# Cross attention: the next half's exponentials ahead of rounding on ScalarE, its normalisation ahead of splitting on VectorE

## What is computed

```python
q_r = einsum('bshq,hqr->bhsr', rope((layernorm(x) @ Wq.T) @ w_kc_q), W_qr)
k_r = einsum('bld,hdr->bhlr', kv_r, W_kr)          # kv_r: the rotated context
attn = softmax(einsum('bhsr,bhlr->bhsl', q_r, k_r), axis=-1)
ctx_c = einsum('bhsl,bld->bhsd', attn, kv_r)
x = x + (einsum('bhsd,hkd->bhsk', ctx_c, w_kc_kv) -> heads side by side) @ Wo.T
```

## Time and profile before

| | us |
|---|---|
| median of 3 runs | 1657.17 |
| lowest, highest | 1654.75, 1658.53 |
| the profiled execution's own time | 1657.46 |
| its span | 1655.7 |
| TensorE busy in the span | 1485.7 (90%) |
| VectorE, ScalarE, GpSimd busy | 1126.5, 810.0, 541.2 |

### The profile page before, as it was taken

The page is one execution under the profiler, slowest core; times in us unless marked ns, Lnnn a source line. Parts: engine busy times, 40 slices in busy tenths (PEclk is TensorE's granted clock), DMA queues, the critical chain, the costliest instruction groups (busy, mean ns, idle before and its releaser), DMA issues. The chain is left out here.

```text
span 1655.7 us, 26391 instructions
## 1 busy us (share of the span) xinstructions
PE 1485.7 (90%) x8136; PEld 1127.4 (68%) x8136; DVE 1126.5 (68%) x1814; ACT 810.0 (49%) x1723; POOL 541.2 (33%) x594
## 2 busy tenths in 40 slices
PE   5799999999946999999999978999899499999996
PEld 3577777777634777777777767887444277777775
DVE  6788878787435878788787854777558436474646
ACT  4556665666423555555555534555210355545453
POOL 4235424341024454545545413220131402221202
PEclk9899999999968999999999998999899699999998
DMA  4132433423267353445444404000444000000000
GB/s 156 59 104 82 126 103 106 125 76 111 78 170 247 106 127 103 120 109 120 112 117 111 129 20 166 0 0 1 154 176 153 0 1 1 26 1 25 1 26 26
DMA packets 140459, 143.78 MB, mean 87 GB/s; under 512 B 83441, under 2 KB 103025, under 8 KB 138737
## 3 DMA queue, kind: packets, MB, share of 16 engines
q1 hardware_dynamic: 138672, 133.87, 27.6%
q10 hardware_dynamic: 1728, 9.20, 1.7%
HBM read 113.54 MB, written 29.49 MB: 86 GB/s over the span
## 5 line engine op out<-in xcount | busy, mean ns | idle before, releaser
L942 ACT ACTIVATE c_e_t_high<-c_et_ps 128x512 fp32r<-128x512 f32 x128 | 76.7, 599 | 227.2 <-PE c_et_ps L1011 227.2
L820 POOL TENSOR_TENSOR c_mixed_low<-c_whole,c_mixed_high 128x512 fp32r<-128x512 f32 x64 | 95.6, 1494 | 178.6 <-ACT c_mixed_high L954 178.6
L77 DVE TENSOR_TENSOR b_rot_parts_low<-b_rot,b_rot_parts_high 128x1536 fp32r<-128x1536 f32 x64 | 135.8, 2122 | 21.8 <-ACT b_rot_parts_high L526 21.8
L1003 PE MATMUL c_sc_ps<-c_kv_t,c_q 128*128 128x257 f32 x512 | 137.1, 392 | 15.1 <-DMA c_q<-carried_queries 15.1
L843 DVE TENSOR_REDUCE c_peak<-c_sc_ps 128x2 f32<-128x514 f32 x128 | 88.5, 691 | 55.7 <-PE c_sc_ps L1003 55.0
L264 POOL TENSOR_TENSOR b_turned_raw<-b_turn_part 128x384 f32<-128x384 f32 x32 | 70.1, 2189 | 166.1 <-DVE b_key_parts_low L77 164.8
L1003 PEld LDWEIGHTS c_sc_ps<-c_kv_t,c_q 128*128 128x128 f32 x512 | 100.1, 197 | 34.5 <-DMA c_q<-carried_queries 15.9
L70 PE MATMUL e_mm_ps<-folded_high,e_h_t_high 128*128 128x512 f32 x256 | 108.8, 425 | 15.8 <-DVE e_h_t_low L77 15.6
L309 DVE TENSOR_TENSOR b_rot<-b_w_qr,b_angle 128x1536 f32<-128x1536 f32 x64 | 119.2, 1863 | 0.2
L1515 PE MATMUL f_ps<-f_right,f_left 128*128 128x512 f32 x256 | 112.6, 602 | 7.3 <-POOL spare L1487 5.0
L934 ACT ACTIVATE c_e<-c_sc_ps,c_peak 128x257 f32<-128x257 f32 x256 | 118.8, 475 | 0.0
(11 more groups left out here) (210 smaller groups left out, 3953.3 us busy)
## 6 DMA issues: line engine op xcount, KB each, us to landing
c_q<-carried_queries SPq DMA_DIRECT2D x64, 256.0 KB, 3.7
c_ends_spread<-end_weights SPq DMA_DIRECT2D x64, 256.0 KB, 4.4
carried_queries<-x SPq DMA_DIRECT2D x7, 2048.0 KB, 11.2
b_early<-early SPq DMA_DIRECT2D x15, 640.0 KB, 4.0
c_raw<-cache_t SPq DMA_DIRECT2D x64, 128.5 KB, 3.9
c_swapped<-cache_t SPq DMA_DIRECT2D x128, 64.2 KB, 3.9
f_left<-ent_in SPq DMA_DIRECT2D x16, 512.0 KB, 5.5
f_right<-ent_out SPq DMA_DIRECT2D x16, 512.0 KB, 6.8
```

Source lines behind the costliest of these rows:

```text
L77: return nc.vector.tensor_tensor(low, value, high.bitcast(F32), ALU.subtract)
L820: nc.gpsimd.tensor_tensor(mixed[1][:, w, :, u], whole[:, u % 2].rearrange("p (h s) -> p h s", h=H), mixed[0][:, w, :, u].bitcast(F32), ALU ...
L1003: last = nc.tensor.matmul(sc_ps[:, 2 * half + c, 0:L], q[:, u, at], kv_t[:, u], start=True, stop=True)
```

## The change

Two calls are moved, each within its engine's step. No instruction, wait or buffer is added or removed. On VectorE `normalise(n + 1)` goes from behind `split_turned(n)`, `split_kv` and `add_out` to ahead of them. On ScalarE `exponential(n + 1)` goes ahead of `round_turned(n)`.

```diff
--- before.py
+++ after.py
@@ -891,13 +891,13 @@
                         find_peak(n + 1, 1 - half)
                     if half == 1 and (u or known(i, 1)):
                         add_end(i - (u == 0), (u - 1) % BT)
+                    if more:
+                        normalise(n + 1, 1 - half)
                     split_turned(n, u, half)
                     if half == 0:
                         split_kv(b, u)
                     if j == 2 and known(i, 2):
                         add_out(i - 2)
-                    if more:
-                        normalise(n + 1, 1 - half)
                     if j == 4 and known(i, 2):
                         keep_moments(i - 2)
 
@@ -967,9 +967,9 @@
                 for j in range(STEPS):
                     n, u, half = STEPS * i + j, j // 2, j % 2
                     b = BT * i + u
-                    round_turned(n, b, u, half)
                     if not (isinstance(n, int) and n == PAIRS - 1):
                         exponential(n + 1, 1 - half)
+                    round_turned(n, b, u, half)
                     if half == 0:
                         round_kv(b, u)
                     if half == 1 and (u or known(i, 1)):
```

## The result

The changed kernel takes **1653.36 us** (median of 20 runs, 1650.56 to 1655.69) against 1657.39 before (median of 20 runs beside it): a ratio of 0.9976, interval 0.9969 to 0.9983, so 4.0 us faster, between 2.8 and 5.1. Forecast were 1651 us and 6.6 us. The profiled execution took 1651.63 us, its span is 1649.8. Two of the 20 executions of before took 2194 and 2195 us and one of even_only's 2807; such slow executions are in the medians and in no ratio.

A forecast was written before the change was run, and what follows sets the result against it. TensorE was taken to set the pace, losing 1.69 us per tile waiting ahead of odd steps' transposes. A gain of 0.47 x 14 = 6.6 us from 1657.46 gave 1651 us, range 1645 to 1661 (8 in 10).

The forecast's parts named there:

- the stall of j = 3: Wait ahead of j = 3's transposes, 0.99 us before; forecast to move to j = 4 as 0.76.
- the walk: Step-by-step clocking of the engines from a step's scores; gave 1.34 us lost per tile before, 1.06 after.
- first case: Stall moves from j = 3 to j = 4, small waits change sides: gain 4.5 to 10.1 us, chance 0.67.
- a new wait of 0.10: Ahead of even steps' transposes, which odd steps' VectorE chain makes 0.10 us late.
- the base of 28.12: Length in us of a tile's four even and four odd steps undisturbed, against 29.81 measured.
- the middle between 0.32 and 0.63: Gain per tile, 0.47 us: 0.32 if lengthened products stay as costly, 0.63 if no longer in the way.
- the 0.31: Loss per tile in us beyond the 1.38 accounted for, put down to lengthened products of line 850.
- the third rival: Even steps' product hits GpSimd's line 803 soon after it begins: slower, deciding from overlap 0.36; chance 0.11.
- The spare of 0.06: VectorE's margin in us in even steps: free that much before the next peaks are wanted.
- The second: Rival: 0.10 more lateness in each of four odd steps leaves 1 us gain, 1656; chance 0.15.
- The fourth: Rival: walk too strict for add_out, TensorE's gaps close: 24 us gain, 1633; chance 0.07.

The follow-up runs named there:

- even_only: Changed kernel with the new order in even steps alone, odd steps in the old order on VectorE and ScalarE: 1649.74 us, ratio 0.9958 to the kernel before.
- act_only: Kernel before with ScalarE's move alone, exponential ahead of round_turned: 1735.34 us, ratio 1.0464.
- dve_only: Changed kernel with ScalarE's two calls as before, so VectorE's move alone: 1687.36 us, ratio 1.0178 to the kernel before.
- wait_swap: Changed kernel with TensorE's two waits ahead of the transposes swapped, low part first: 1652.20 us, ratio 0.9971 to the kernel before.
- wait_first: Changed kernel with those two TensorE waits swapped and an always-met wait for the pair's scores ahead: 1652.85 us, ratio 0.9975 to the kernel before.
- gap_after: Changed kernel with add_out right behind find_peak at j = 2 and the output product shifted a step: 1646.33 us, ratio 0.9935 to the kernel before.
- kv_gap: Kernel before with split_kv behind the normalisation and add_out behind the peaks, ScalarE's order old: 1633.87 us, ratio 0.9858.

## Why the prediction was right, and where its sum was off

*The mechanism* was as forecast. The waits of odd steps went, small ones ahead of even steps' transposes came, and the stall of j = 3 moved to `add_out`'s next victims. In ordinary steps the starts on VectorE agree with the walk within 0.01, those on ScalarE within 0.02. That neither move does it alone, act_only and dve_only show. Where the gain comes from was half right. The prediction had two sources, `add_out` (0.99 to 0.76) and smaller waits in the other steps; the first came (0.96 to 0.77), the second did not (0.67 to 0.69). And the gain of 4.0 us lies below the 4.5 to 10.1 that the prediction gave for its first case.

*"The transposes 4.40. They are wanted at 3.43 + 0.87 = 4.30: a new wait of 0.10"* was the mis-sized term: it measured 0.23. The handover from the end of `c_e_t_low` to the transposes is 0.14 to 0.16, where I had taken the product's 0.05 (755.40 to 755.45) for it. The product's signal is the first of the two waits in TensorE's stream, the low part's the second, and wait_swap and wait_first show that the place makes a difference; and an odd step without a wait is 3.39 long (753.42 - 750.03), not 3.43, so TensorE comes 0.04 earlier. Four such steps a tile: with 0.77 at j = 3 and 4 against 0.76 forecast, the tile loses 1.45 against the base of 28.12 where 1.06 were forecast. The 0.39 between them is three times 0.13.

*`add_out`*: the total was right (0.50 + 0.27 = 0.77 against 0.76), but by luck. It holds the step's own wait, 0.23 and not 0.10, so that `add_out`'s part is 0.54 and not 0.66 (0.47 by gap_after's period): the even step was the longer for its wait and gave VectorE that much more time. Its form was not foreseen either. Of the lateness 0.27 is spent already ahead of the first output product of j = 3, which waits for `c_out_ps` to be emptied. The prediction didn't name that wait. gap_after removes both, and 7 us with them.

*The lengthened products.* I took the middle between 0.32 and 0.63; the upper end was the truth, since no lengthened product makes a transpose of the changed kernel late (all odd steps 0.00), and 0.63 - 0.39 = 0.24 is the measured gain per tile (29.81 - 29.57). But the 0.31 that set the two ends apart was not all lengthened products. In the kernel before these lasted 0.71, 0.72 and 0.87 at j = 0, 4 and 6 over tiles 3 to 13, 0.23 above three times 0.69. The other 0.08 came at j = 0, where ScalarE's rounding and all behind it begin 0.08 later (1.59 behind the scores of 758.01 instead of 1.51); why was not looked into. Products of even steps do pay to line 803, up to 0.94 us:

```profile
741.50 0.64 POOL L803 TENSOR_TENSOR c_part<-c_swapped,c_table 128x257 f32<-128x257 f32 x1
```

```profile
741.75 0.94 DVE L850 TENSOR_TENSOR c_e<-c_e,c_inverse 128x512 f32<-128x512 f32 x1
742.61 0.68 DVE L77 TENSOR_TENSOR c_e_t_low<-c_et_ps,c_e_t_high 128x512 fp32r<-128x512 f32 x1
743.21 0.41 DVE L77 TENSOR_TENSOR c_kv_low<-c_kv_ps,c_kv_high 128x256 fp32r<-128x256 f32 x1
...
743.85 0.69 DVE L843 TENSOR_REDUCE c_peak<-c_sc_ps 128x2 f32<-128x514 f32 x1
```

The overlap is 742.14 - 741.75 = 0.39, more than the 0.26 forecast and above the 0.36 from which the third rival was to decide. It decided nothing: the peaks behind it start at 743.85, 1.07 after their scores (742.78), on time. The even step had been made 0.23 longer by its own wait, which gave VectorE the time. The spare of 0.06 had been computed with too short a wait, and the two errors covered each other.

The Trainium skill, page "SBUF — State Buffer", section "SBUF: two separate sides", has the second of two such instructions wait out the first. The durations here agree with a small credit: 0.14 of the overlap is free at 0.34, at 0.39 and at 1.04, and the first one is not lengthened. All eleven traces say the same: 422 products began 0.17 to 1.05 ahead of the end of a GpSimd operation, and each was lengthened by that overlap less 0.13 to 0.16.

*The sum.* 14 tiles at 0.24 are 3.4 us. The first two tiles, put at nothing, were 1.5 shorter in the profiled executions (76.9 against 75.4 us from the first scores to those of the third tile). But wait_swap and wait_first, with the changed kernel's orders on VectorE and ScalarE, have 74.8 and 76.8 there, so that the 1.5 is not shown to be the change's. The whole stage, from the first scores to the last transposes, shrank from 491.8 to 486.7 us; another 1.2 of the profiled difference lies ahead of the stage, where nothing was changed. The runs say 4.0, between 2.8 and 5.1.

*The rivals.* The second (nothing measurable) was close: its condition, 0.10 more lateness per odd step, came true with 0.13, and what kept the gain was that the lengthened products went. The third's mechanism is real: act_only pays for it beside line 820, even_only beside line 803. The fourth was right in the prize and wrong in the way to it: all of TensorE's gaps can be closed, but by taking `add_out` and `split_kv` out of the chain (kv_gap), not by this change.

What stays open is the law of the handover: four values were seen for four places of the wait, and no cost per wait or register instruction was found that fits all of them. In the time none of it could be told apart.

## What to carry to other kernels

Before two chains are swapped, write down for each wait of the bounding engine which operations stand ahead of its releaser without being needed by it. Here they were `split_kv`, which waits for ScalarE, and `add_out`, 0.34 and 0.82 us of slots; putting just these behind the releaser or into an idle gap gave 23 us, where letting the next pair pass the whole of the present one gave 4, because that put another needed operation, `c_e_t_low`, last. Here such a swap lost 30 and 78 us when only one of the two engines of the chain made it. And when adding up a chain with margins near 0.1 us, take each handover from a row in which the same wait, in its place in the stream, is the last to be met.

## What was not expected of the hardware

Two elementwise instructions, a product of VectorE with both inputs in SBUF and one on GpSimd, cost the later one the overlap less 0.14 us over a wide range (0.34, 0.39, 1.04 us of overlap; 0.20, 0.25, 0.89 us of lengthening); the traces hold 780 cases with GpSimd as the later one, with 0.15 to 0.66 us of overlap, and they differ from this by 0.02 at most. `c_e_t_low`, which reads one of its inputs from PSUM, was not lengthened beside line 820 or 808: 59 of them ran whole beside line 820 and lasted no more than 0.69. The time from the end of VectorE's instruction to the start of the transposes that waited for it was 0.05 to 0.16 us in these runs, and it changed with the place of the wait among TensorE's waits, also behind the same instruction.
